# Routing done per batch inside the gated unit, a shorter ranking, and the first expert tile by one-hot products

## What is computed

```python
x = x + xattn(layernorm(x), ctx)      # 16 heads, 2048 context rows, bias by relative position
x = x + attn(layernorm(x), ...)       # retention, group norm, then the gated unit:
#   h2  = rmsnorm(x, ln2_w)
#   mlp = silu(h2 @ gate_w.T) * (h2 @ up_w.T) @ down_w.T      # inner width 1408
x = x + ffn(layernorm(x), ...)        # eight experts, each token goes to one of them:
#   logits = x @ w_router + b_router                           # 512 x 8
#   top1   = argmax(softmax(logits))
#   out    = sum over e of where(top1 == e, gelu(x @ w1[e] + b1[e]) @ w2[e] + b2[e], 0)   # 512 -> 2048 -> 512
```

## Time and profile before

| | us |
|---|---|
| median of 3 runs (range) | 2012.06 (2011.84 to 2013.36) |
| the profiled execution, its own time | 2014.59 |
| its span, first to last instruction | 2012.8 |

### The profile page before, as it was taken

The page is one execution under the profiler, slowest core; times in us unless marked ns, Lnnn a source line. Parts: engine busy times, 40 slices in busy tenths (PEclk is TensorE's granted clock), DMA queues, the critical chain, the costliest instruction groups (busy, mean ns, idle before and its releaser), DMA issues. The chain is left out here.

```text
span 2012.8 us, 40993 instructions
## 1 busy us (share of the span) xinstructions
PE 1881.8 (93%) x17262; PEld 1442.8 (72%) x17262; DVE 1131.3 (56%) x2161; ACT 777.8 (39%) x1294; POOL 806.4 (40%) x641
## 2 busy tenths in 40 slices
PE   7999999999999999999999998599779997599995
PEld 6777777777777777777777776477567876599995
DVE  4536556556556556556556567745755233355553
ACT  3224443443443443343343334421244220366663
POOL 2117776776776776776776762000000000100001
PEclk9999999999999999999999999899889996799998
DMA  6122122122122122122122202020040006799993
GB/s 206 55 88 74 30 78 74 34 78 74 33 80 74 33 79 75 33 80 74 33 80 69 80 2 70 2 88 1 1 152 21 1 1 227 270 366 358 360 359 108
DMA packets 107672, 201.44 MB, mean 100 GB/s; under 512 B 8960, under 2 KB 46144, under 8 KB 102384
## 3 DMA queue, kind: packets, MB, share of 16 engines
q1 hardware_dynamic: 106032, 194.60, 28.8%
q0 software_dynamic: 1472, 4.40, 0.7%
HBM read 184.54 MB, written 14.44 MB: 99 GB/s over the span
## 5 line engine op out<-in xcount | busy, mean ns | idle before, releaser
L303 POOL TENSOR_TENSOR z<-z,probT 128x512 f32<-128x512 f32 x392 | 503.9, 1285 | 232.0 <-ACT probT L351 207.8
L456 DVE TENSOR_REDUCE negm<-bank 128x1 f32<-128x512 f32 x512 | 326.8, 685 | 181.7 <-PE bank L651 177.3
L437 DVE TENSOR_TENSOR probT<-bank,z 128x512 f32<-128x512 f32 (+1 forms) x512 | 291.1, 615 | 211.8 <-PE bank L663 211.8
L351 ACT ACTIVATE probT<-probT 128x1024 f32<-128x1024 f32 x256 | 271.1, 1059 | 230.3 <-DVE probT L437 217.5
L345 ACT ACTIVATE v<-bank 128x512 f32<-128x512 f32 x128 | 76.4, 597 | 474.4 <-PE bank L626 474.4
L279 POOL TENSOR_TENSOR h_lo<-ctx_raw,h_hi 128x512 fp32r<-128x512 f32 x124 | 160.7, 1296 | 170.9 <-ACT h_hi L328 167.3
L681 PEld LDWEIGHTS bank<-probT,v 128*32 128x32 f32 x4096 | 104.0, 109 | 93.7 <-ACT probT L351 92.3
L626 PE MATMUL bank<-h_hi,w_hi 128*128 128x512 f32 x512 | 152.7, 420 | 11.3 <-ACT h_hi L328 11.3
L663 PEld LDWEIGHTS bank<-q,k 32*128 32x128 f32 x4096 | 126.0, 186 | 46.6 <-issue 44.3
L626 PE MATMUL bank<-w_hi,h_hi 128*128 128x512 f32 x512 | 152.3, 419 | 0.0
L663 PE MATMUL bank<-q,k 32*128 32x128 f32 x4096 | 150.2, 283 | 0.5 <-DVE probT L437 0.5
(11 more groups left out here) (240 smaller groups left out, 2802.1 us busy)
## 6 DMA issues: line engine op xcount, KB each, us to landing
w_sb<-w SPq DMA_DIRECT2D x10, 4096.0 KB, 13.9
w_sb<-w SPq DMA_DIRECT2D x40, 1024.0 KB, 6.0
x_res<-bias_table SPq DMA_DIRECT2D x64, 512.0 KB, 5.1
ctx_raw<-ctxT SPq DMA_DIRECT2D x124, 256.0 KB, 3.2
slots<-zero_sb SPq DMA_DIRECT2D x17, 256.0 KB, 3.0
down_w<-down SPq DMA_DIRECT2D x11, 256.0 KB, 2.7
xslot<-slots SPq DMA_DIRECT2D x11, 256.0 KB, 9.2
b_sb<-b SPq DMA_DIRECT2D x10, 256.0 KB, 6.5
```

What stands on the lines that cost most here:

```text
L303: pool.tensor_tensor(total[:, g], total[:, g], part, ALU.add).then_inc(add_step, 1)
L351: act.activation(pT[:, u % 2, j:j + 2], pT[:, u % 2, j:j + 2], ACT.Exp).then_inc(exp_done, 1)
L437: dve.tensor_tensor(pT[:, u % 2, j, i0:], sc[:, i0:], shift[:, g, j].unsqueeze(1).broadcast_to([P, ST - i0, T]), ALU.add).then_inc(shifted, 1)
L456: dve.tensor_reduce(negm[:, c, h:h + 1], sc[:], AX.X, ALU.max, negate=True).then_inc(max_done, 1)
```

## The change

glu_phase takes over the first part of routing, route_phase is gone, and the rest stands at the head of expert_phase.

1. In glu_phase, the seam between the halves: `turn(4)`, `turn(5)`, `narrow(0)`, `turn(6)`, `turn(7)`, `narrow(1)` to `narrow(3)`. `narrow` of a half's first batch waits for ten lo parts at its start and for the eleventh only at i = 10.
2. For batches 0 to 3 the mean and variance, the normalisation, the transposes (`flip`, into bank 0), the copy and the product with the router's weights (`logits`, into bank 1) lie in the second loop (moments at i = 0 and 1, square root at 2, reciprocal and normalisation at 3 and 4, transposes on PE after i = 4 to 7, logits after i = 5 to 8). For batches 4 to 6 they lie in the `narrow` of the next batch, at i = 7, with the logits one batch later; `logits(6)`, `flip(7)` and `logits(7)` come after the last `narrow`.
3. POOL zeroes, and SP stores the zeroes, during the gated unit; SP also loads the seven small inputs and w1 of expert 0 there. w2 of expert 0 is loaded at the head of expert_phase.
4. Ranking: the counts over batches are accumulated in PSUM, with 8 products for the total (bank 3) and then 8 for the ranks (bank 2), in place of 2 products and 8 additions; the sums over experts are one product with a triangular table and one reduction in place of 8 additions.
5. The first tile's transposed rows come from `pick_first`: 32 float32 products of `xn` with one-hot matrices `spot`, made by DVE with one comparison per batch. The scatter to DRAM stays; SP waits for it (`x_out`) before it reads tile 1 and loads w1 of tile 1's expert, and waits for `pick_first` too, since this w1 is put where `xn` lies.
6. One SBUF tensor `arena` holds, phase by phase, v, z, the raw weights, w1 and the routing's small tensors.

```diff
+                def narrow(b):
+                    if b >= 2:
+                        pe.wait_ge(down_out, b - 1)
+                    for i in range(IT):
+                        if b > HALF and i == 7:
+                            if b > HALF + 1:
+                                logits(b - 2)
+                            flip(b - 1)
+                        if b % HALF == 0 and i in (0, IT - 1):
+                            pe.wait_ge(a_lo_done, b // HALF * IT + (IT - 1 if i == 0 else IT))
+                            pe.wait_ge(down_lo_done, IT)
...
                         mm.then_inc(up_mm, 1)
+                        if half and 5 <= i < 5 + HALF:
+                            logits(i - 5)
+                        if half and 4 <= i < 4 + HALF:
+                            flip(i - 4)
                     if half == 0:
-                        turn(1)
-                    narrow(half)
+                        turn(HALF)
+                        turn(HALF + 1)
+                        narrow(0)
+                        turn(HALF + 2)
+                        turn(HALF + 3)
+                        for b in range(1, HALF):
+                            narrow(b)
+                    else:
+                        for b in range(HALF, B):
+                            narrow(b)
+                        logits(B - 2)
+                        flip(B - 1)
+                        logits(B - 1)
...
+                def roots(b0, b1):
+                    act.wait_ge(moment_step, 2 * b1 + 1)
+                    act.activation(small[:, 0, b0:b1], mv[:, b0:b1, 1], ACT.Sqrt, bias=feps[:]).then_inc(root, 1)
...
+                        if half and i == 2:
+                            roots(0, HALF)
...
+                for b in range(HALF, B):
+                    narrowed(b)
+                    moment(b)
+                    invert(b, b + 1)
+                    normal(b)
+                    keep_turned(b)
...
+                sp.wait_ge(zeroed, 1)
+                for k in range(MT + 1):
+                    sp.dma_start(env["xs_dram"][k * P:(k + 1) * P, :], zero).then_inc(zero_out, 16)
+                sp.wait_ge(gu_lo_done, 2 * IT)
+                for n, at, size in ROUTE_INPUTS:
+                    rows = env[n] if n == "before_in" else env[n].unsqueeze(0).broadcast_to([P, size])
+                    sp.dma_start(arena[:, at:at + size], rows).then_inc(env["route_in"], 16)
+                sp.wait_ge(zero_out, 16 * (MT + 1))
+                load_w1(sp, env, 0, 0)
```

At the head of expert_phase (its DVE steps run one behind the other as before):

```diff
-                sp.dma_start(xs[:], env["xs_dram"][0:P, :]).then_inc(xs_in, 16)
+                load_b1(sp, env, 0, 0)
+                for q in range(Q):
+                    load_w2(sp, env, 0, q)
+                load_b2(sp, env, 0, 0)
+                sp.wait_ge(x_out, 16 * B)
+                rows(1)
+                sp.wait_ge(v_step, ROUTED)
+                sp.wait_ge(turned, 1)
                 e = expert_of(sp, env, 1)
                 load_w1(sp, env, e, 1)
                 load_b1(sp, env, e, 1)
...
+                def ranks():
+                    pe.wait_ge(ones_set, 1)
+                    pe.wait_ge(v_step, MINE)
+                    for b in range(B):
+                        mm = pe.matmul(bank[3][:, 0:E], ones, mine[:, b, :], start=(b == 0), stop=(b == B - 1))
+                    mm.then_inc(rank_mm, 1)
+                    pe.matmul(bank[2][:, 0:B * E], before, mine, start=True, stop=False)
+                    for b in range(B - 1):
+                        mm = pe.matmul(bank[2][:, (b + 1) * E:B * E], ones,
+                                       mine[:, b, :].unsqueeze(1).broadcast_to([P, B - 1 - b, E]), start=False,
+                                       stop=(b == B - 2))
+                    mm.then_inc(rank_mm, 1)
+
+                def pick_first():
+                    for c in range(DC):
+                        for b in range(B):
+                            if c == 0:
+                                pe.wait_ge(spot_done, b + 1)
+                            mm = pe.matmul(bank[0][:, c * P:(c + 1) * P], xn[:, b, c * P:(c + 1) * P], spot[:, b, :],
+                                           start=(b == 0), stop=(b == B - 1))
+                    mm.then_inc(turned, 1)
+
+                ranks()
+                pick_first()
-                turn(0)
                 tile(0, 0, 0)
```

More of the change, by code:

```diff
@@ L1307, in _ @@
+                for b in range(HALF):
+                    turn(b)
                 for half in range(2):
@@ L1559, in expert_phase, with part, by_token @@
         y = sb("y", [P, D])
-        back = w1[:].rearrange("p s c n -> p (s c n)")[:, 0:B * D].rearrange("p (b d) -> p b d", b=B)
+        def part(at, size):
+            return arena[:, at:at + size]
+        def by_token(at):
+            return part(at, B * E).rearrange("p (b e) -> p b e", b=B)
+        before, iota, br, index, starts, tiles, lower = [part(at, size) for _, at, size in ROUTE_INPUTS]
+        lower = lower.rearrange("p (e f) -> p e f", e=E)
+        ones = part(4352, P)
+        spot = part(4608, B * P).rearrange("p (b t) -> p b t", b=B)
+        logit, hit, mine, pos = [by_token(5632 + i * B * E) for i in range(4)]
+        top, first, slot_f, count, ntile, base, upto = [part(5888 + i * E, E) for i in range(7)]
+        over = part(5952, E * E).rearrange("p (e f) -> p e f", e=E)
+        past = part(6016, MT * E).rearrange("p (m e) -> p m e", m=MT)
+        te = part(6144, MT)
+        last_tile = sb("last_tile", [P, 1], I32)
+        v_step, ones_set, rank_mm, spot_done, x_out = (sem("f_v_step"), sem("f_ones"), sem("f_rank_mm"),
+                                                       sem("f_spot"), sem("f_x_out"))
+        MINE, SLOTS, ROUTED = 6, 17, 24
+        back = w1[0].rearrange("p c n -> p (c n)")[:, 0:B * D].rearrange("p (b d) -> p b d", b=B)
         xs_in = sem("e_xs_in")
@@ L1776, in build @@
         env["last_pair"] = ctx.enter_context(nc.sbuf_tensor("last_pair", [P, 1], I32))
[L1778 to L1779 removed]
+        for name, shape in (("w2_sb", [P, FT, D]), ("b1_sb", [P, 2, FT]), ("b2_sb", [P, 2, D])):
             env[name] = ctx.enter_context(nc.sbuf_tensor(name, shape, F32))
[L1781 to L1783 removed]
         expert_phase(nc, env)
```

400 lines of the change are left out of this document (177 added, 223 removed).

## The result

| | before | after |
|---|---|---|
| median of 4 runs (range) | 2012.60 (2011.84 to 2013.36) | 1984.62 (1982.20 to 1987.14) |
| the profiled execution, its own time | 2014.59 | 1984.76 |
| its span | 2012.8 | 1982.9 |

The ratio is 0.9861 (95% interval 0.9844 to 0.9878): 28.0 us sooner by the medians, 29.9 by the spans. Forecast were 1978.8 and 33.3 sooner; the time lies within the range of 1972 to 1988, 5.8 us above its middle case (28.0 are counted from the median of four, the forecast from the earlier median of three, 2012.06).

What follows compares the result with a forecast made beforehand. PE bounds the experts, and routing is a chain of hand-overs, so starting the first widen earlier shortens the total. 31.8 us sooner plus 1.5 of clock gave 33.3, so 1981.3, less 2.5 for the median: 1978.8, range 1972 to 1988.

Steps and rivals of the forecast that it cites:

- Seam: Gated unit: narrow(0) starts 5.3 us sooner, net -5.0; second narrow loses its wait and low clock, -4.7.
- Second loop: Gated unit's second loop: four flips and four logits add 5.2 us on PE; DVE's added work is hidden by idle time.
- Table load: ACT in the second loop: loading the root's table and going back delays 0 to 0.4 us, taken as 0.4.
- The chain behind the last add: From DVE's last add to the first widen: 26.6 us, so widen starts 31.8 us sooner.
- The first `widen` at 2.4 GHz: First tile of the experts: PE, busy with pick_first just before, starts widen at 2.4 GHz, 1.5 us more gained.
- The weights: Experts: w1(1) issued at 32.5 us, landing 5.9 us before widen(1) needs it; later loads unchanged, tiles stay 25.63 apart.
- rival C: w1(1) late: scatter or the 4 MB take over 5.9 us longer; at 10 us longer, +4, 1983; chance 0.06.
- The step from spans to the median: Whole kernel: the median lies 2.5 us below the profiled execution, so 1981.3 becomes 1978.8.
- A: PE's clock lasts through logits(6), flip(7) and the ranks, -4.3, and pick_first lacks its slow start, -1.5: 1973; chance 0.10.
- B: PE's clock comes late: pick_first runs at 1.2 GHz throughout and widen starts slow, +5.0 + 1.5: 1985; chance 0.09.
- D: Small products pull the clock down inside the gated unit from block 4 on: +60, 2039; chance 0.03.
- E: The new chain is longer than laid out, by added DVE and PE instructions or stalls at flips: +8, 1987; chance 0.05.

Runs made afterwards that it cites:

- the 32 bytes: Kernel after the change with 32 unused bytes per partition ahead of down_hi, so h2T_hi and h2T_lo begin at a multiple of 64 bytes again: 1980.33 us.
- the seam alone: Kernel before with only the gated unit's new order at both seams and the eleventh lo part waited for at i = 10: 2003.35 us, ratio 0.9959.
- the kernel before with the 32 bytes: Kernel before with 32 unused bytes per partition ahead of down_hi, putting it and the operands behind it at 32 modulo 64 bytes: 2013.12 us, ratio 1.0003.
- seam undone: Kernel after the change with the old order at both seams and narrow waiting for all eleven lo parts at its start: 1995.76 us.

## Why the prediction was right, and where its sizes were off

The direction, the mechanism and the range held. The size was 33.3 for spans that differ by 29.9, and the 3.4 between them divide up by the table (the start of the gated unit 0.4 later, the rest from a to h):

- *Seam*, forecast -5.0 and, for the second `narrow`, -4.7. From the first pair of transposes to `narrow(0)` are 2.18 us where it was 7.40, 5.22 less (forecast 5.3); stretch a fell by 4.95, since its first loop is 0.27 longer. b rose by 0.21 (forecast 0.3). `down_lo` was late next, as said. The runs give 10.0 and 8.85 for both terms together, where 9.7 was forecast: right. The two differ mostly by the 1.7 of low clock behind the second wait, which comes in some executions only.
- *Second loop*, +5.2 for the small PE work, forecast for c 62.80 - 2.96 + 5.6 = 65.4. It took 66.78. With the 32 bytes it is 65.19; against the seam alone (59.84) the small work costs 5.35. The term was right; what failed is the step before it, "a block is 24 products, 5.44 us", taken over from before unchanged. Item 6 of the change moved tensors, and the blocks became 5.6. By the products' spacing that is 1.75 a loop (264 x 0.0066); of it 1.6 were measured in c. The first loop, in which PE waits for weights between blocks, shows 0.4 to 0.8. With the start 0.4 and this, the last add came at 1677.59 where 1675.4 was forecast.
- *Table load*, 0 to 0.4, taken as 0.4. The load for the root lay in ACT's idle time. The one back held silu 0.35 us: it starts 5.95 us behind the silu before it, where the blocks are 5.60 apart:

```profile
1591.99 1.28 ACT L1234 ACT_TABLE_LOAD   x1
...
1593.29 0.30 ACT L1234 ACTIVATE fsmall<-fmv,feps 128x4 f32<-128x4 f32 x1
...
1593.60 1.28 ACT L1252 ACT_TABLE_LOAD   x1
...
1594.89 0.60 ACT L1252 ACTIVATE glu_prod<-bank 128x512 f32<-128x512 f32 x1
```

  The cover that was counted for it held, and PE lost nothing. The drain of 1.38 us that the Trainium skill ("ScalarE: Activation LUTs", What ACT_TABLE_LOAD costs) adds to a change of set doesn't show: each activation starts within 0.02 us of its load's end, and the second load 0.01 us behind the activation ahead of it.
- *The chain behind the last add*, forecast 26.6, took 25.31. Of the 1.3, 1.2 lie between `flip(7)` and the ranks: the copy started 0.69 us behind the turn, not 1.13, and the ranks at 7.4, not 8.6, since PE still had clock 1.00 in `flip(7)` and 0.91 on the mean from 1681 to 1683, where I had priced both at 1.2 GHz. From there on each term was met: ranks 7.07 (forecast 7.1), `pick_first` and its end 9.0 to the copy (1702.16 - 1693.17; forecast 9.1), `widen` 0.74 later.
- *The first `widen` at 2.4 GHz*, 1.5: f fell by 1.49. Right.
- *The weights.* SP issued w1(1) 30.6 after the last add, forecast 32.5, and `widen(1)` followed on `narrow(0)` with no wait. Right. The next step failed: "From w1(2) on every load waits for the same events of PE and DVE as before, so the loop keeps its 25.63". The events are the same, but `widen(0)` starts 5.2 us ahead of the issue of w1(1) where it started 3.4 behind it. So the rows of tile 2, behind w1(2) on SP's queue, are requested 8.6 us closer to the 4 MB loads of tile 1, and landed 15.5 us after their issue where it was 10.6. g rose by 2.26. This is rival C's place, SP's queue, with other data late than it named. The tiles after have 25.66 each in place of 25.63, 0.3 in all, not explained.
- *The step from spans to the median*, -2.5, failed for 1.9: the kernel before has 2.0 between its profiled execution (2014.59) and its median of four, the kernel after 0.1. It was one execution's place in the spread of the phases ahead, not a constant of the program. So: 3.4 and 1.9 are the 5.3 by which 28.0 falls short of 33.3; the fourth run of the kernel before, which moved its median by 0.5, makes it the 5.8 by which the time is off.

Of the rivals, A (the clock lasts) got its first two steps, `logits(6)` and `flip(7)`, with most of `logits(7)`, and no more: the ranks' 32 records took 0.2135 each, clock 0.50 from 1685 to 1693. B fell: `pick_first` brought the clock to 1.00 by itself (0.68 from 1695 to 1697, 1.00 behind it). D fell: 1.00 throughout the second loop and the second `narrow` stage with all flips in it. The rule that transposes don't count as PE being busy (the Trainium skill, "TensorE: Matmul & The Clock Gate", PE-mode transpose) had nothing to decide here. E fell, the chain was shorter.

What the parts are worth, then: the seam 8.9 to 10.0; `pick_first` 8.6, of which the wait for the rows takes 1.1 to 2.3 back; the new ranking -0.6; the offsets -2.0 to -2.4. Routing's work moved under the gated unit is the rest: e fell by 31.9, 7.0 of it by `pick_first` and against 0.6 from the ranking, and c and d pay 8.5 for what moved in (5.35 and 3.15 over the kernel with the seam only), which leaves some 17. That share is got by subtraction; the move itself was not measured alone.

## What to carry to other kernels

When a chain is shortened, look at which requests now meet on a queue, and put the small ones that gate the engine first. When a change moves buffers, compare the time per product of the loops whose work it leaves alone. And price a stage behind an idle engine with the clock that the profile grants there, knowing that part of a stage's saving comes back as low clock in the next.

## What was not expected of the hardware

- The time of a float32r product of 512 columns depends on where its operands lie: 0.2267 us with both at the same offset within 64 bytes, 0.2333 with one on 64 and one 32 beyond (three kernels, both directions), and in one execution of such a layout 0.267 through most of a loop at clock 1.00. That last value is not explained.
- The same wait of 2.8 us was followed by a lower clock in three executions (d 31.87 in the kernel before, whose next product took 0.76) and not in two (d 30.25 in the kernel before with the 32 bytes; next product 0.50). The next product alone doesn't tell: it took 0.47 with seam undone, whose clock was 0.50 from 1.2 us behind it.
- At 1.2 GHz a float32 product of 8 columns costs two records of 0.21 to 0.22, and so do products of 64 and of 56 down to 8 columns (16 records in 3.56 us, 14 in 3.10; a merged one saved 3.0 us in the ranks): merging narrow products saves, narrowing them doesn't.
- Four products that nobody reads, put into PE's waits, took 3.0 us out of the chain (stretch e, 23.55 to 20.52); the medians differ by 1.3, with overlapping intervals.
